# Normalising and choice weights moved into the experts' turns, prefix counts summed on TensorE, places found by quarters

## What is computed

```python
xn = _layernorm(x, axis=-1)
x = x + _L0_attn_ref(xn, ...) + _L0_ffn_ref(xn, ...)
```

```python
topk_w, topk_i = lax.top_k(masked_scores, K)
topk_w = topk_w / (topk_w.sum(axis=-1, keepdims=True) + 1e-08)
routed = jnp.einsum('eti,ehi,te->th', h, ed_w, comb)
```

## Time and profile before

| what | us |
|---|---|
| median of the three runs | 3993.14 |
| span of the profiled execution | 3993.6 |
| route block, to the first work of the next | 0 to 128.6 |
| recurrence and shared expert | 128.6 to 419.4 |
| routed experts | 419.4 to 877.7 |
| combine | 877.7 to about 960 |
| second layer | to the end |

### The profile page before, as it was taken

How to read it: one execution, slowest core, us unless ns; L and a number is a source line. 1 busy time by engine, 2 the same in 40 slices (tenths; PEclk the granted TensorE clock), 3 DMA queues, 4 the chain that set the end, 5 groups by cost and what they waited for, 6 DMA issues and landing times.

```text
span 3993.6 us, 72415 instructions
## 1 busy us (share of the span) xinstructions
PE 3555.5 (89%) x26059; PEld 3107.7 (78%) x26059; DVE 3278.4 (82%) x3459; ACT 1974.7 (49%) x2535; POOL 3344.8 (84%) x1502
## 2 busy tenths in 40 slices
PE   5593699977599999999999999999999999999999
PEld 4252688866388888888888888888888888888888
DVE  8536555547699999899999999998999999999988
ACT  1010233344265555655555565555555555655555
POOL 1678455541699999999999999999999999999997
PEclk8696899998799999999999999999999999999999
DMA  9322456669000000000000000000000000000000
GB/s 381 110 103 77 143 181 191 187 211 335 15 5 5 8 5 5 5 5 5 5 5 6 6 5 8 5 5 5 5 5 6 5 5 6 5 8 5 5 5 5
DMA packets 110620, 209.18 MB, mean 52 GB/s; under 512 B 16608, under 2 KB 77280, under 8 KB 110304
## 3 DMA queue, kind: packets, MB, share of 16 engines
q1 hardware_dynamic: 84192, 140.90, 11.0%
q0 software_dynamic: 21504, 59.93, 4.1%
q10 hardware_dynamic: 4608, 4.20, 0.3%
HBM read 183.34 MB, written 107.74 MB: 73 GB/s over the span
## 4 chain that ended last, share of the span: by engine, by line
PE 58%; DVE 7%; issue 4%; ACT 2%; POOL 2%; DVEq 0%; ACTq 0%; DMA 0%; POOLq 0%
PE at_num L1483 21%; PE at_den L1483 19%; PE at_work L1461 9%; PE at_work L1471 4%; DVE at_pv L1169 2%; PE at_misc L1509 2%; POOL at_s L1250 2%; DVE at_k_low L1396 2%; PE at_misc L1515 2%; ACT at_s L1329 1%; DVE at_s L1169 1%; PE at_work L1462 1%; DVE at_k_top L1393 1%; DVE at_pv L1170 1%; ACT at_k_far L1270 1%
## 5 line engine op out<-in xcount | busy, mean ns | idle before, releaser
L1250 POOL TENSOR_TENSOR at_s<-at_s,at_m 128x2048 f32<-128x2048 f32 (+7 forms) x768 | 2511.3, 3306 | 31.0 <-DVE at_s L1169 22.9
L1329 ACT ACTIVATE at_s<-at_s 128x2048 f32<-128x2048 f32 (+7 forms) x768 | 1080.7, 1418 | 611.5 <-POOL at_s L1250 611.2
L1483 PE MATMUL at_den<-k_ident,at_s 128*128 128x128 f32 x9216 | 1135.2, 273 | 54.0 <-ACT at_s L1329 52.5
L1483 PE MATMUL at_num<-k_ident,at_pv 128*128 128x128 f32 x9216 | 1142.8, 274 | 0.5 <-DVE at_pv L1170 0.5
L1483 PEld LDWEIGHTS at_num<-k_ident,at_pv 128*128 128x128 f32 x9216 | 1049.9, 142 | 91.2 <-issue 69.3
L1483 PEld LDWEIGHTS at_den<-k_ident,at_s 128*128 128x128 f32 x9216 | 1037.0, 141 | 85.7 <-ACT at_s L1329 60.0
L1170 DVE TENSOR_TENSOR at_pv<-at_s,at_vp 128x2048 f32<-128x2048 f32 (+7 forms) x512 | 692.1, 1352 | 229.9 <-ACT at_vp L1304 179.9
L1170 DVE TENSOR_TENSOR at_s<-at_q,at_kp 128x2048 f32<-128x2048 f32 (+7 forms) x512 | 691.6, 1351 | 14.2 <-ACT at_kp L1299 9.4
L1169 DVE TENSOR_TENSOR at_pv<-at_s,at_vp 128x2048 f32<-128x2048 f32 x256 | 584.8, 2284 | 0.0
L1169 DVE TENSOR_TENSOR at_s<-at_q,at_kp 128x2048 f32<-128x2048 f32 x256 | 582.1, 2274 | 0.0
L1461 PE MATMUL at_work<-k_region,at_xT 128*128 128x512 f32 x788 | 408.2, 644 | 105.6 <-ACT at_k_far L1270 81.7
(11 more groups left out here) (235 smaller groups left out, 3557.7 us busy)
## 6 DMA issues: line engine op xcount, KB each, us to landing
moe_w<-experts SPq DMA_DIRECT2D x256, 384.0 KB
slot_x<-k_region SPq DMA_DIRECT2D x16, 2144.0 KB, 25.2
moe_x<-slot_x SPq DMA_DIRECT2D x256, 134.0 KB, 3.3
cmb_y<-picked SPq DMA_DIRECT2D x32, 768.0 KB, 8.5
at_xT<-xT SPq DMA_DIRECT2D x33, 128.0 KB, 2.2
e_x<-u SPq DMA_DIRECT2D x4, 1024.0 KB, 9.5
picked<-moe_yo,moe_row POOLq DMA_INDIRECT x256, 3.2
xT<-cmb_xT ACTq DMA_DIRECT2D x32, 128.0 KB, 5.9
```

Of the source, the lines that this page charges most:

```text
L1250: nc.gpsimd.tensor_tensor(part(s_slot, c), part(s_slot, c), by_query(m[unit_of(c)][:], c), ALU.subtract).then_inc(sub_done, 1)
L1329: nc.scalar.activation(part(s_slot, c), part(s_slot, c), ACT.Exp, scale=C ** -0.5).then_inc(exp_done, 1)
L1483: ins = nc.tensor.matmul(dst[:, b * P:(b + 1) * P], buf[:, at:at + P], k.ident[:], start=(c in (0, NTRI) and x == 0 and b == 0), stop=Fals ...
```

## The change

- `select` stops after `sel`, now bfloat16; its scaling of the chosen scores is gone, and with it `k.comb`.
- TensorE sums the tiles' counts. With bfloat16 copies of `k.ones` and `k.upper` (made once on VectorE at the start) it adds every tile of a quarter into `total` (8 products of 64 columns), the counts within tiles into `cum[q]` (512 columns), and on top of them each tile's count onto the tiles behind it: 7 products of 448 down to 64 columns in its own quarter, and 8 products of 512 columns for every later quarter. It starts on this when all scores are done.
- VectorE waits for `total`, works out the blocks from it, and then calls `place(q)` for each quarter: add, mask, search, the row's tail, and the slots. `slots_done` is counted up after the first quarter, and GpSimd scatters two tiles (`EARLY_TILES = 2`) in the route block.
- In the next block GpSimd only scatters the other 30 tiles; both `normalise` halves and the making of the choice weights are gone from it.
- GpSimd takes all inverse roots at the start of `routed_experts`. VectorE gets `finish(n, step)`, ten instructions for tile n in turn n, dealt over the turn by `FINISH`; its loop is written out in 32 turns.
- `combine` has its own `xn`, and `choice_w` has the tile ahead of the choice.

```diff
-EARLY_TILES = 1
+EARLY_TILES = 2
...
-                pool.wait_ge(masks, 4)
...
+                def onto(q, first, n, start, stop):
+
+                    times = QUARTER - first
+                    return nc.tensor.matmul(cum[q][:, first:QUARTER, :], ones_b[:],
+                                            view(sel[:], [[0, times], [1, E]], n * E), start=start, stop=stop,
+                                            skip_group_check=True)
+
+                pe.wait_ge(evacuated, NT)
+                pe.wait_ge(score_done, 4)
+                pe.wait_ge(rounded, 2)
                 for q in range(4):
                     pe.wait_ge(sel_done, q + 1)
-                    nc.tensor.matmul(cum[q], k.upper[:], sel[:, tiles(q), :], start=True, stop=True)
-                    nc.tensor.matmul(all_[q], k.ones[:], sel[:, tiles(q), :], start=True, stop=True).then_inc(cum_done, 1)
+                    mine = range(q * QUARTER, (q + 1) * QUARTER)
+                    for n in mine:
+                        ins = nc.tensor.matmul(total, ones_b[:], sel[:, n, :], start=(n == 0), stop=(n == NT - 1),
+                                               skip_group_check=True)
+                    ins.then_inc(total_done, 1)
+                    nc.tensor.matmul(cum[q], upper_b[:], sel[:, tiles(q), :], start=(q == 0), stop=False,
+                                     skip_group_check=True)
+                    for i in range(QUARTER - 1):
+                        ins = onto(q, i + 1, mine[i], False, i == QUARTER - 2)
+                    ins.then_inc(cum_done, 1)
+                    for later in range(q + 1, 4):
+                        for n in mine:
+                            onto(later, 0, n, n == 0, False)
...
-                    c(v.tensor_tensor(cb, sel[:, tiles(q), :], ms, ALU.mult))
-                    c(v.tensor_reduce(small[:], cb, AX.X, ALU.add))
-                    c(v.tensor_scalar(small[:], small[:], 1e-8, None, ALU.add))
-                    c(v.reciprocal(small[:], small[:]))
-                    c(v.tensor_tensor(cb, cb, view(small[:], [[1, QUARTER], [0, E]]), ALU.mult))
...
+                def place(q):
+
+                    dve.wait_ge(cum_done, q + 1)
+                    nm = number[:, tiles(q), :]
+                    c(v.tensor_tensor(nm, cum[q], view(base[:], [[0, QUARTER], [1, E]]), ALU.add))
+                    c(v.tensor_tensor(nm, nm, sel[:, tiles(q), :], ALU.mult))
+                    for n in range(q * QUARTER, (q + 1) * QUARTER):
+                        c.mark(v.max(top8[:, n, :], number[:, n, :]))
...
+                    v.tensor_scalar(k.slot[:, tiles(q), :], top8[:, tiles(q), :], -1.0, None, ALU.add
+                                    ).then_inc(slots_done, 1)
...
-                c = Chain(pool, pool_step)
-                for g, (low, high) in enumerate(((EARLY_TILES, ROOT_AT), (ROOT_AT, NT))):
-                    scatter_tiles(nc, k, scratch, range(low, high))
-                    pool.wait_ge(moments, (g + 1) * NT // 2)
...
+                scatter_tiles(nc, k, scratch, range(EARLY_TILES, NT))
                 pool.wait_ge(scattered, 16 * NT * TOPK)
...
-                normalise(0)
-                chosen = hs[:].rearrange("p b (n e) -> p (b n) e", e=E)
-                for j in range(TOPK):
-                    c(v.tensor_tensor(chosen, k.key[:], view(k.top8[:], [[8, NT], [0, E]], j), ALU.is_equal))
-                    c(v.tensor_tensor(chosen, chosen, k.comb[:], ALU.mult))
-                    c(v.tensor_reduce(k.choice_w[:, j, :], chosen, AX.X, ALU.add))
-                normalise(1)
-                c.join()
+                dve.wait_ge(moments, NT)
+                dve.wait_ge(sy_free, NT)
...
+                FINISH, STEPS = {2: (0, 1), 3: (2, 3), 5: (4, 5), 6: (6, 7), 7: (8, 9)}, 10
...
+                    if step >= 2:
+                        dve.wait_ge(finished, n * STEPS + (step - 1 if step <= 5 else step))
...
+                    if step == 0:
+                        dve.wait_ge(roots_done, 1)
+                        ins = v.tensor_scalar(xs, xs, k.mv[:, n, 0:1], k.rstd[:, n:n + 1], ALU.subtract, ALU.mult)
+                    elif step == 1:
+                        ins = v.tensor_tensor(match[:], view(k.number[:, n, :], [[0, TOPK], [1, E]]),
+                                              view(k.top8[:, n, :], [[1, TOPK], [0, E]]), ALU.is_equal)
+                    elif step == 2:
+                        ins = v.tensor_tensor(xs, xs, k.gamma, ALU.mult)
+                    elif step == 3:
+                        ins = v.tensor_tensor(match[:], match[:], view(k.key[:, n, :], [[0, TOPK], [1, E]]), ALU.mult)
+                    elif step == 4:
+                        ins = v.tensor_tensor(x, x, xs, ALU.add)
+                    elif step == 5:
+                        ins = v.tensor_reduce(w6, match[:], AX.X, ALU.add)
+                    elif step == 6:
+                        ins = v.tensor_reduce(norm[:], w6, AX.X, ALU.add)
+                    elif step == 7:
+                        ins = v.tensor_scalar(norm[:], norm[:], 1e-8, None, ALU.add)
+                    elif step == 8:
+                        ins = v.reciprocal(norm[:], norm[:])
+                    else:
+                        ins = v.tensor_scalar(w6, w6, norm[:], None, ALU.mult)
...
+                        for step in FINISH.get(j, ()):
+                            finish(i, step)
...
-                for i in range(2):
-                    turn(i, i)
-                with dve.Fori(1, TURNS // 2) as i:
-                    for u in range(2):
-                        turn(i * 2 + u, u)
+                for i in range(TURNS):
+                    turn(i, i % 2)
```

122 lines of the change are left out of this document (54 added, 68 removed).

## The result

The changed kernel takes 3949.06 us (median of 4 runs, 3945.66 to 3952.16) against 3993.22 us for the kernel before on the same chip (3992.79 to 3994.1): a ratio of 0.989, 95% interval 0.9878 to 0.9901. The prediction, 3953 us in a range of 3932 to 3978 and faster with a chance of 0.85, held. It held partly by luck: terms of its sum were off in opposite directions, which the experiments sort out.

What follows compares the result with a forecast made beforehand. VectorE's tail, 343 to 419 us, was taken to be on the path before the experts. Removing it and starting scatters earlier wins 54 us, finishing steps cost 14: 3993.6 - 54 + 14 = 3953.6, less 0.5: 3953 us, range 3932 to 3978.

Steps and rivals of the forecast that it cites:

- Selection, counts, slots: Route block: last `sel` at 83.9, 0.8 us wait for counts, 3.4 us placing a quarter, first slots at 89.6.
- Rival 2, TensorE late: Route block: TensorE's counts come 36 us late, GpSimd starts 20 us later than forecast; 3973 us, chance 0.07.
- The fill sets GpSimd's start: Before the first scatter: last zero fill lands at 105.8, GpSimd starts at about 106.0; only 13.0 of 29.1 us count.
- GpSimd becomes the bound of the recurrence's block: Recurrence block: VectorE's work ends at 338.5, GpSimd's scatters run on, the last starting at 359.4.
- The handover: From recurrence to experts: 6.6 us after the last scatter's start, so experts begin at 366.0, 54 us won.
- The roots: Start of the experts' block: GpSimd takes roots for 32 tiles, some 5 us, at no cost.
- The finishing steps: Experts' turns: ten VectorE instructions, 3.7 us a turn; TensorE held up 0.9 to 1.3, 0.45 felt, 14 us in all.
- The written-out loop: VectorE's loop over the experts' turns: no effect either way; bounds together with `combine` -5 to +5 us.
- The sum: Whole kernel: 3993.6 - 54 + 14 = 3953.6, less 0.5, gives 3953 us; chance 0.66.
- Rival 1, VectorE sets the turn: Experts' turns: all 3.7 us of finishing steps felt each turn, +117 - 54 = +63, 4056 us; chance 0.10.
- Rival 3, all absorbed: Experts' turns: waits for rows swallow the finishing steps' hold-up, felt 0 a turn, 3939 us; chance 0.12.
- Rival 4, pauses of the stream: VectorE's written-out program: pauses like one 3.4 us gap seen on GpSimd, 12 times, 3990 us; chance 0.05.

Runs made afterwards that it cites:

- e7: Changed kernel with two further 2 MB zero transfers that GpSimd's first scatter also waits for; 3956.08 us, ratio 0.9914.
- e3: Changed kernel with EARLY_TILES at 0, so all 192 scatters stand in the recurrence's block; 3947.01 us, ratio 0.9887.
- e5: Changed experts' block with the tail moved into its turns, behind the old route block of the kernel before; 3956.06 us, ratio 0.9916.
- e10: Changed kernel run again without edit, on another chip; 3948.86 us, ratio 0.9891.
- e1: Changed kernel without its ten finishing steps a turn, choice weights all 1/6, loop still written out; 3937.46 us, ratio 0.9867.
- e6: Changed kernel's route block, but the tail in the recurrence's block as before, and the written-out loop without finishing steps; 3980.96 us, ratio 0.9981.
- e8: Changed kernel with all ten finishing steps of a turn at j = 5 instead of spread over five places; 4067.07 us, ratio 1.0197.

## Why the prediction was right, step by step

- **Selection, counts, slots.** The last `sel` at 83.3 (said: 83.9), the wait for the total 0.70 us (0.8), the first slots at 88.6 (89.6). Placing a quarter takes 3.04 us, from one start of L347 to the next, not 3.4. Each within a microsecond, and none of it on the path.
- **Rival 2, TensorE late.** It stood at 7% and is refuted: the first quarter's 31 products, 14,080 columns in all, took 7.47 us, where the bfloat16 row would give 11.3. That row was rightly chosen over the float32 one, and even it was too dear.
- **The fill sets GpSimd's start.** Said 106.0, measured 106.98, with the fill as releaser. e7 shows it by moving the fill. Reading kept a false gain of 16 us out of the forecast: whoever follows only VectorE's slots forecasts a start at 89.6.
- **GpSimd becomes the bound of the recurrence's block.** Said: VectorE ends at 338.5 and the last scatter starts at 359.4; measured 338.3 and 360.81. Of the 1.4 us one is the fill's. e3, e5 and e7 each move this chain, by 3.1 us earlier and by 12 and 9.5 later, and the experts' begin follows by 2.1, 12.8 and 9.4.
- **The handover: wrong by 1.8 us.** I took the 6.6 us of the earlier trace rows; from the start of the last scatter to the next block it took 8.4, in e3 9.4. That is the term that was mis-sized; with the 1.4 us of the line above it makes the begin 369.2 instead of 366.0, and the gain 50.2 us instead of 54. The rows of the border show where they lie: the forecast took over the experts' end, where GpSimd's DRAIN takes 3.65 us, and here it takes 5.52, which is 1.87 more; in e3 it takes 6.51. Its last DMA activity ends 2.1 us behind the last scatter's start. Why a DRAIN is longer in one block than in another is open: it grows by 0.99 us from 180 scatters in the block to 192 (6.01 with the 186 of e5), but behind the 256 of the experts it is the shortest, and behind the 186 of the kernel before, with the roots among them, it takes 7.70.
- **The roots.** 5.47 us from 369.83 on, with no engine waiting for them: nothing, as said.
- **The finishing steps: right in the hold-up by luck, wrong in parts.** Said: a hold-up of 0.9 us at j = 5, half of it swallowed by the waits for rows, 0.45 felt, 14 us. Measured: a hold-up of 0.44 us in the median turn, because the copy comes only 0.42 us later than before, not 0.9: operations follow each other by less than their length (0.34 and 0.46 us for steps 4 and 5, 0.80 in sum), and the pause of 0.3 us behind the finding of rows is gone with the hardware loop. The 0.44 is so near to the 0.45 by chance, since it comes about another way. And of those 13.6 us little is swallowed: the waits at j = 4 are 20.5 us in e10, 24.3 and 23.0 without steps, so 2.5 to 3.8 us. The steps cost 9.3 us (the mean of 460.6 less 451.3, the mean of e1 and e6).
- **The written-out loop.** Taken as nothing within 5 us; the traces put it at 2.2 to 4.1 us of gain, inside that bound and not clear of their spread, and 3.5 more are open. Together with the steps the stretch grows by 2.7 us in the mean, 6.9 in the first trace, not by 14.
- **The sum.** 54 less 14 made 40 us; it was 50.2 less 6.9, and 3.1 of chance behind it: 46.4. The first term was over by 4 us, the second by 7, and 3 came by chance. The 46.4 us are the difference of two profiled spans; the medians differ by 44.2. In every run whose time is listed beside its span the time lies 1.7 to 2.2 us above it, so by this estimate the execution behind the 3993.6 took some 3995.5 us, 2 more than its kernel's median.
- **Rival 1, VectorE sets the turn.** The kernel as made does not show it. e8 shows that its mechanism is real, though with the chain at one j and not at every one: heaped at j = 5 the steps lengthen the stretch by 119 us against e1 and e6, 3.7 us a turn (569.9 less 451.3, over 32), twice the 1.7 us from which it decides. That this meets the rival's 117 us is luck: some 90 are the hold-up (31 times 2.9) and most of the rest is the clock's, which the rival did not have. Spread the steps cost 0.3 us a turn. That the steps were spread is what makes the change pay.
- **Rival 3, all absorbed**, is refuted by the 0.44 us a turn; its number, 3939 us, is 10 us below the measured one. **Rival 4, pauses of the stream**: VectorE's stream shows no such pauses, and the traces point to a gain.

## What to carry to other kernels

Before moving work beside another engine's chain, ask at each place how late the next hand-off may come, not how idle the engine is: the same ten operations cost 9 us spread over five places and over 100 at one. What is won on one engine counts only up to the next releaser; here 18 of the 30 us by which the slots came earlier ended in a wait for a fill, and only once the tail was gone did the other 12 arrive whole. Take the price of a block's end from a block that ends as yours will, and look at the rows of the border itself. And a hold-up of TensorE can cost more than its own length where the clock falls after it.

## What the runs showed of the hardware that was not expected

- A wait of 2.6 us in TensorE's stream, once a turn, was followed in most turns of e8 by a granted clock of 0.50 (1.2 GHz) for the next round: 1.3 us more a turn; in 7 of 31 turns the clock stayed at 1.00. Hold-ups of 0.44 us were not followed by it: in the changed kernel the granted clock is 1.00 from 390 to 815 us.
- A GpSimd scatter takes 0.96 us alone and up to 1.35 beside a two-input operation of VectorE of only 0.55 us; with the finishing steps beside them the 256 took 24.9 us more.
- A block that ends on a scatter hands over 8.4 to 9.4 us behind the start of its last one here, and 6.6 at another place of the same program. Most of it is GpSimd's DRAIN: 5.5 to 6.5 us here, 3.65 there.
- In a hardware loop VectorE paused 0.3 us at a step with several waits; written out, the same step followed without a pause in nearly all turns.
